# An order of VectorE's work written anew in a four-stage scan, and GpSimd's first operations of a step behind one more wait

## The reference

```python
def _derivative(q, p, drive, coupling, bias):
    i_couple = jnp.tanh(q) @ coupling.T
    dq = q - q ** 3 / 3.0 - p + drive + i_couple + bias
    dp = EPSILON * (q + ALPHA - BETA * p)
    return (dq, dp)
def _rk4_step(q, p, drive, coupling, bias):
    dq1, dp1 = _derivative(q, p, drive, coupling, bias)
    dq2, dp2 = _derivative(q + 0.5 * DT * dq1, p + 0.5 * DT * dp1, drive, coupling, bias)
    dq3, dp3 = _derivative(q + 0.5 * DT * dq2, p + 0.5 * DT * dp2, drive, coupling, bias)
    dq4, dp4 = _derivative(q + DT * dq3, p + DT * dp3, drive, coupling, bias)
    q_next = q + DT / 6.0 * (dq1 + 2 * dq2 + 2 * dq3 + dq4)
    p_next = p + DT / 6.0 * (dp1 + 2 * dp2 + 2 * dp3 + dp4)
    q_next = jnp.clip(q_next, -CLAMP, CLAMP)
    p_next = jnp.clip(p_next, -CLAMP, CLAMP)
    return (q_next, p_next)
```

## Time and profile before

| what | value |
|---|---|
| median of 3 runs | 5511.95 us |
| the profiled execution itself | 5501.18 us |
| its span (first to last instruction) | 5499.4 us |
| TensorE busy | 4413.1 us, 80% |
| VectorE busy | 4183.3 us, 76% |
| ScalarE busy | 2305.9 us, 42% |
| GpSimd busy | 1722.9 us, 31% |

### The profile page before, as it was taken

How to read it: one execution, slowest core, us unless ns; L and a number is a source line. 1 busy time by engine, 2 the same in 40 slices (tenths; PEclk the granted TensorE clock), 3 DMA queues, 4 the chain that set the end, 5 groups by cost and what they waited for, 6 DMA issues and landing times. The chain is left out here.

```text
span 5499.4 us, 212720 instructions
## 1 busy us (share of the span) xinstructions
PE 4413.1 (80%) x78665; PEld 3812.1 (69%) x78665; DVE 4183.3 (76%) x25970; ACT 2305.9 (42%) x10514; POOL 1722.9 (31%) x5965
## 2 busy tenths in 40 slices
PE   6777777777777777777776787699999999969999
PEld 5666666666666666666665566578777787758777
DVE  7999999999999999999995667377777777631123
ACT  3333333333333333333333566255555555432243
POOL 2444444444444444444443221123333323100000
PEclk5555555555555555555557999699999999989999
DMA  2000000000000000000002000322222222131121
GB/s 70 1 1 1 1 1 1 1 1 1 1 1 1 1 1 1 1 1 1 1 1 78 32 21 17 117 73 73 81 76 85 81 74 65 46 137 47 39 100 39
DMA packets 145838, 187.93 MB, mean 34 GB/s; under 512 B 9372, under 2 KB 75492, under 8 KB 145288
## 3 DMA queue, kind: packets, MB, share of 16 engines
q1 hardware_dynamic: 140800, 182.67, 10.0%
q0 software_dynamic: 624, 0.75, 0.1%
q10 hardware_dynamic: 3992, 0.17, 0.0%
HBM read 143.67 MB, written 39.90 MB: 33 GB/s over the span
## 5 line engine op out<-in xcount | busy, mean ns | idle before, releaser
L211 PE MATMUL bank<-tanh_parts,w_lo 128*128 128x4 f16 x32768 | 1208.3, 169 | 756.6 <-ACT tanh_parts L168 755.4
L211 PEld LDWEIGHTS bank<-tanh_parts,w_lo 128*128 128x128 f16 x32768 | 1033.6, 105 | 941.5 <-ACT tanh_parts L168 940.5
L168 ACT ACTIVATE tanh_parts<-ys 128x8 f16<-128x8 f32 x4096 | 857.5, 209 | 1801.2 <-DVE ys L298 1800.2
L219 PE MATMUL bank<-tanh_parts,w_hi 128*128 128x8 f16 x32768 | 1200.7, 173 | 2.9 <-issue 2.9
L219 PEld LDWEIGHTS bank<-tanh_parts,w_hi 128*128 128x128 f16 x32768 | 1059.5, 104 | 3.0 <-issue 3.0
L298 DVE TENSOR_TENSOR_SCAN ys<-mix,bank 128x24 f32<-128x24 f32 x4096 | 805.4, 202 | 125.3 <-PE bank L219 25.3
L169 ACT ACTIVATE tanh_full<-ys 128x8 f32<-128x8 f32 x4096 | 804.0, 196 | 0.0
L290 DVE TENSOR_TENSOR tanh_parts<-tanh_full,tanh_parts 128x8 f16<-128x8 f32 x4096 | 704.0, 172 | 1.3 <-ACT tanh_full L169 0.7
L1256 POOL TENSOR_TENSOR t_w_qk<-t_raw_qk,t_w_qk 128x512 fp32r<-128x512 f32 x128 | 168.1, 1335 | 765.0 <-ACT t_w_qk L1420 765.0
L475 PE MATMUL t_bank<-t_x,t_w_qk 128*128 128x512 f32 x1536 | 361.5, 391 | 12.8 <-DVE t_x L1676 12.8
L475 PEld LDWEIGHTS t_bank<-t_x,t_w_qk 128*128 128x128 f32 x1536 | 290.1, 189 | 73.9 <-DVE t_x L1676 13.5
(11 more groups left out here) (232 smaller groups left out, 9103.6 us busy)
## 6 DMA issues: line engine op xcount, KB each, us to landing
t_raw_qk<-L_cond_qkv_w_dram SPq DMA_DIRECT2D x128, 256.0 KB, 3.3
t_raw_vo<-L_cond_qkv_w_dram SPq DMA_DIRECT2D x16, 1024.0 KB, 5.1
t_raw_vo<-L_cond_out_w_dram SPq DMA_DIRECT2D x16, 1024.0 KB, 5.3
n<-t_parts SPq DMA_DIRECT2D x14, 1024.0 KB, 6.6
g_raw<-L_cond_ffn_w_dram SPq DMA_DIRECT2D x8, 1024.0 KB, 9.9
g_x<-n SPq DMA_DIRECT2D x8, 1024.0 KB, 8.7
ada_w<-L_cond_ada_w_dram SPq DMA_DIRECT2D x4, 1536.0 KB, 10.7
t_x<-n SPq DMA_DIRECT2D x6, 1024.0 KB, 6.9
```

Of the source, the lines that this page charges most:

```text
L168: act.activation(tanh_parts[:, u, at, :, 0], ys[:, s, at, :, 2], ACT.Tanh, scale=1.0 / SCALE).then_inc(s_th, 1)
L211: pe.matmul(sums[:, :, 2], w_lo[:, w_of, k, m * P:(m + 1) * P], tanh_parts[:, u, k, :, 0], start=(m % 2 == 0 and k == 0), stop=False, skip ...
L219: last = pe.matmul(sums[:, :, 1:3], w_hi[:, w_of, k, m * P:(m + 1) * P], tanh_parts[:, u, k], start=False, stop=(m % 2 == 1 and k == C - 1 ...
```

## The change

On VectorE:

- Stage 0: `known` (net times H plus q) is no longer worked out ahead of the base. The gain is folded into `cub` and `slope`, so the base is net times H plus slope. `known_0` is made at the start of stage 1 instead.
- Stage 1: the two parts of `known`, `rate`, `third_1` and `p_2` change places; `rate` now stands behind the base. `twice` goes between the two scans, and the third `known` to the start of stage 2.
- Stage 3: `rate_3` stands ahead of `cub`; the last `thirds` is folded into `slope`, and the base becomes a `tensor_tensor` of slope and known. The clip of p moves from between the two scans to before them.
- `result`: the wait for the base is written behind the wait for `s_mm`, and in stages 0, 1 and 3.
- 45 instructions per step in place of 46.

On GpSimd: the first product `gq` waits for `s_rate` as well (the rate of stage 0), and with it the second product, the trace copy and the sum behind it.

```diff
@@ -98,7 +98,7 @@
         slope = sb("slope", [P, C, B], F32)
         known = sb("known", [P, STAGES, C, B], F32)
         twice = sb("twice", [P, C, B], F32)
-        thirds = sb("thirds", [P, STAGES, C, B], F32)
+        thirds = sb("thirds", [P, STAGES - 1, C, B], F32)

         mix = sb("mix", [P, C, B, 3], F32)
         gq = sb("gq", [P, 2, C, B], F32)
@@ -295,38 +295,38 @@
                 u, to = s % 2, (s + 1) % STAGES
                 for half, at in enumerate(HALVES):
                     v.wait_ge(s_mm, t * 2 * STAGES + (2 * s + half + 1))
+                    if half == 0 and s != 2:
+                        after("base")
                     v.tensor_tensor_scan(ys[:, to, at].rearrange("p c b n -> p (c b n)"), mix[:, at].rearrange("p c b n -> p (c b n)"),
                                          banks[2 * u + half][:, 0:C // 2 * B * 3], 0.0, ALU.mult, ALU.add).then_inc(s_q, 1)
                     if half == 0 and between is not None:
                         between()

-            def cubed(y):
-                own("cub", stt(cub[:, :, :], y, -1.0 / (3.0 * SCALE * SCALE), y, ALU.mult, ALU.mult))
-
-            def sloped(y):
+            def cubed(y, gain=1.0):
+                own("cub", stt(cub[:, :, :], y, -gain / (3.0 * SCALE * SCALE), y, ALU.mult, ALU.mult))
+
+            def sloped(y, first=1.0):
                 after("cub")
-                own("slope", stt(slope[:, :, :], cub[:, :, :], 1.0, y, ALU.add, ALU.mult))
+                own("slope", stt(slope[:, :, :], cub[:, :, :], first, y, ALU.add, ALU.mult))

             def based(s, of):
                 own("base", stt(mix[:, :, :, 1], slope[:, :, :], GAIN[s], of))

             y1, y2, y3 = [ys[:, s, :, :, 2] for s in (1, 2, 3)]
+

             def stage_0(t):
                 v.wait_ge(s_q, t * 2 * STAGES + 2)
                 v.tensor_scalar(q[:, :, :], ys[:, 0, :, :, 2], -CLAMP * SCALE, CLAMP * SCALE, ALU.max, ALU.min).then_inc(s_clip, 1)
                 low_part(t, 0, 0)
                 v.wait_ge(s_clip, t + 1)
-                cubed(q[:, :, :])
+                cubed(q[:, :, :], GAIN[0])
                 low_part(t, 0, 1)
+                sloped(q[:, :, :], 1.0 + GAIN[0])
                 v.wait_ge(s_net, t + 1)
-                own("known", stt(known[:, 0], net[:, :, :], H, q[:, :, :]))
-                sloped(q[:, :, :])
-                v.wait_ge(s_p, t + 1)
                 stt(rate[:, 0], p[:, :, :], -BETA, q[:, :, :]).then_inc(s_rate, 1)
                 after("slope")
-                based(0, known[:, 0])
-                after("base")
+                own("base", stt(mix[:, :, :, 1], net[:, :, :], H, slope[:, :, :]))

                 def between():
                     v.wait_ge(s_rate, t * 3 + 1)
@@ -334,37 +334,35 @@
                 result(t, 0, between)

             def stage_1(t):
-                own("known", stt(known[:, 1], rate[:, 0], -EPSILON * H * H, known[:, 0]))
+                own("known_0", stt(known[:, 0], net[:, :, :], H, q[:, :, :]))
                 v.wait_ge(s_q, t * 2 * STAGES + 4)
                 cubed(y1)
-                after("p_1")
-                stt(rate[:, 1], ps_[:, 1], -BETA, y1).then_inc(s_rate, 1)
+                after("known_0")
+                own("known", stt(known[:, 1], rate[:, 0], -EPSILON * H * H, known[:, 0]))
                 low_part(t, 1, 0)
                 sloped(y1)
                 low_part(t, 1, 1)
                 after("slope")
                 based(1, known[:, 1])
+                stt(rate[:, 1], ps_[:, 1], -BETA, y1).then_inc(s_rate, 1)
+                v.wait_ge(s_third, t + 1)
+                own("third_1", stt(thirds[:, 1], y1, THIRD, thirds[:, 0]))
                 v.wait_ge(s_rate, t * 3 + 2)
                 own("p_2", stt(ps_[:, 2], rate[:, 1], EPSILON * H, p[:, :, :]))
-                v.wait_ge(s_third, t + 1)
-                own("third_1", stt(thirds[:, 1], y1, THIRD, thirds[:, 0]))
-                after("base")
-                own("twice", stt(twice[:, :, :], net[:, :, :], 2 * H, q[:, :, :]))

                 def between():
-                    after("twice")
-                    own("known", stt(known[:, 2], rate[:, 1], -2 * EPSILON * H * H, twice[:, :, :]))
+                    own("twice", stt(twice[:, :, :], net[:, :, :], 2 * H, q[:, :, :]))
                 result(t, 1, between)

             def stage_2(t):
+                after("twice")
+                own("known", stt(known[:, 2], rate[:, 1], -2 * EPSILON * H * H, twice[:, :, :]))
                 v.wait_ge(s_q, t * 2 * STAGES + 6)
                 cubed(y2)
-                after("p_2")
                 stt(rate[:, 2], ps_[:, 2], -BETA, y2).then_inc(s_rate, 1)
                 low_part(t, 2, 0)
                 sloped(y2)
                 low_part(t, 2, 1)
-                after("third_1")
                 own("third_2", stt(thirds[:, 2], y2, 2 * THIRD, thirds[:, 1]))
                 after("slope")
                 based(2, known[:, 2])
@@ -376,24 +374,19 @@

             def stage_3(t):
                 v.wait_ge(s_q, t * 2 * STAGES + 8)
-                cubed(y3)
                 own("rate_3", stt(rate[:, 3], ps_[:, 3], -BETA, y3))
+                cubed(y3, GAIN[3])
                 low_part(t, 3, 0)
-                sloped(y3)
+                sloped(y3, THIRD + GAIN[3])
                 low_part(t, 3, 1)
-                after("late")
-                own("known", stt(thirds[:, 3], y3, THIRD, known[:, 3]))
                 v.wait_ge(s_psum, t + 1)
-                after("rate_3")
                 own("moved", stt(p_new[:, :, :], rate[:, 3], EPSILON * H / 3, p_sum[:, :, :]))
-                after("known")
-                based(3, thirds[:, 3])
-                after("base")
-
-                def between():
-                    v.tensor_scalar(p[:, :, :], p_new[:, :, :], (-CLAMP - SHIFT_P) * SCALE, (CLAMP - SHIFT_P) * SCALE,
-                                    ALU.max, ALU.min).then_inc(s_p, 1)
-                result(t, 3, between)
+                after("slope")
+                own("base", v.tensor_tensor(mix[:, :, :, 1], slope[:, :, :], known[:, 3], ALU.add))
+                after("moved")
+                v.tensor_scalar(p[:, :, :], p_new[:, :, :], (-CLAMP - SHIFT_P) * SCALE, (CLAMP - SHIFT_P) * SCALE,
+                                ALU.max, ALU.min).then_inc(s_p, 1)
+                result(t, 3)

             for t in range(T):
                 stage_0(t)
@@ -435,6 +428,7 @@
                 g.wait_ge(s_p, t + 1)
                 tt(net[:, :, :], drive_now[:, :, :], p[:, :, :], ALU.subtract).then_inc(s_net, 1)
                 g.wait_ge(s_clip, t + 1)
+                g.wait_ge(s_rate, t * 3 + 1)
                 own(tt(gq[:, 0], q[:, :, :], by_rest, ALU.mult))
                 g.wait_ge(s_net, t + 1)
                 of_net = own(tt(gq[:, 1], net[:, :, :], by_third_h, ALU.mult))
```

## The result

The changed kernel takes 5448.72 us (median of 4 runs, 5446.01 to 5453.77) against 5511.47 before (5508.94 to 5513.26): ratio 0.9888, 95% interval 0.987 to 0.9905, 62.8 us less. The forecast was 5439 us in a range of 5419 to 5468.

The account below looks back on a forecast made before the run. The prediction took the scan's ring (scan, tanh, matmuls, scan) at half clock, VectorE 93% busy, as the bound. Terms -69 -13 +12 -3 = -73 us took the profiled 5501.2 to 5428, plus 10.8 gives 5439 us, range 5419 to 5468.

Parts of the forecast that it names:

- The waits: First scans of stages 0 and 3: s_mm rides on the scan, the base wait stands alone at no cost; -69 us.
- The collision in stage 3: With rate_3 first, cub starts level with or ahead of GpSimd's drive_now and escapes its stretch; -13 us.
- The cube at 0.23: Stage 3: cub taking 0.24 us was listed as showing the prediction wrong.
- the first rival: GpSimd strikes more, cub of stage 3 losing to drive_now or cub of stage 1 hit; 5459 to 5475 us, chance 0.2.
- The chain in stage 3: Stage 3: cub 0.09 us later delays slope and low part 1, scan at 1.14 over a floor of 1.12; +12 us.
- Stage 1: A later gp spares low part 1, gain 0.028; hits by GpSimd's moved products cost 0.023 us per step; net -3 us.
- The 46th instruction: VectorE's step: removing one instruction was counted at nothing.
- the slow rivals: Two slower cases: s_mm's wait stands alone, 5543 us, chance 0.04; a full lock, 5531 us, chance 0.03.
- the one by which the lone wait would be that for `s_mm`: First scans of stages 0, 1 and 3: s_mm always gets its own instruction; +31 us, 5543, chance 0.04.
- The full lock: Stage 0: GpSimd's second product holds off p_1 to its end, 0.18 us per step; +92 us, 5531, chance 0.03.
- the ring: The scan phase's repeating chain of each stage: scan, tanh, matmuls, scan.

Follow-up runs that it names:

- e1: The changed kernel with the waits ahead of the first scan of stages 0, 1 and 3 in the old order, base before s_mm: 5555.95 us, ratio 1.0089.
- e4: The kernel before with s_mm written ahead of the base wait in stages 0 and 3, nothing else: 5525.86 us, ratio 1.0031.
- e2: The changed kernel without GpSimd's wait for the rate of stage 0, so VectorE's new order alone: 5477.23 us, ratio 0.995.
- e5: The changed kernel with GpSimd's copy of the next drive waiting until both low parts of stage 3 are written: 5434.40 us, ratio 0.9854.
- e9: The changed kernel with a late drive copy, cub first in stage 3 and the base ahead of moved, 48 entries per step: 5410.09 us, ratio 0.9818.
- e10: The changed kernel with one more wait, for rate_3 ahead of moved, 49 entries per step on VectorE: 5460.81 us, ratio 0.9912.
- e3: The kernel before with GpSimd's wait for the rate of stage 0 and nothing else: 5495.41 us, ratio 0.9968.

## Why the prediction was right, and where it was not

The sum was right to 10 us of 73 by the medians (62.8), to 17 by the stages of the scan (56.3), and its largest term for its reason. The other three terms were wrong and partly made up for each other: two in stage 3 were too good by about 18 and 5 us, the one in stage 1 too bad by 13. That part of the closeness is luck.

- **The waits** (-69). The mechanism is shown by e1. In stage 3 the full 0.07 came (the scan 0.37 behind low part 1, formerly 0.44). Its reason, that the wait written first rides on the instruction, holds in e1, e4 and the changed kernel. In stage 0 the prediction wrote "with the lone wait behind it the scan can go at 2017.17", counting 0.09 from the base to the scan. The four pairs of rows in the changed kernel, e2 and e4 give 0.10 to 0.11. The mean gain of stage 0 is 58 ns instead of 67 and the gain of its median 52, the difference being the vanished stalls. The exchange alone does not bring it: in e4, where the base is as late as before, it costs.
- **The collision in stage 3** (-13). This step failed: "cub starts about 0.01 earlier than rate does now, level with or ahead of the copy, and I expect it to win". I had given the rate a push of 0.09 as in second place; in first place, behind the wait for the state, it pushes the next by 0.10 as cub did (2003.29, 2003.39). cub starts 13 to 14 ns behind the copy, where the rate had started 14 behind it, and was struck in 383 of the 384 steps in which the copy lies there (in every fourth step it comes 0.37 us later). The cube at 0.23 was one of the prediction's own signs of being wrong. That was the first rival's mechanism, given 0.2. Before, the rate was struck in 298 steps, six in ten, so this term was a loss and not a gain: 85 strikes more at the 60 ns by which a struck stage 3 is longer (1447 against 1387) are, by estimate, 5 us. e5 shows what all strikes cost: 46 ns per step.
- **The chain in stage 3** (+12). Right in kind and too small. cub a tenth later makes slope and low part 1 late; in the steps that are not hit stage 3 takes 1387 ns, against 1353 without a lone wait or collision in e9: 34 instead of 23.
- **Stage 1** (-3). It gained 31 ns, 16 us: all that the struck low part 1 had cost and 3 ns more, and the strike on cub or known that I put against it did not come. `thirds` started at 2000.47, 0.10 ahead of cub, which took its usual 0.18.
- **The 46th instruction** "at nothing". Its removal was worth the 6.4 us of the 25 long stages, by the place at which every 128th entry falls (e10). This cost was in the trace of before, in the waits of the scan for TensorE, and I did not ask what they were (the row of `--waits` over the scan):

```profile
DVE ys L298 <- PE bank L219: 22.4, 130, 0.5
```

Of the 130 only 8 belong to long stages, those of 0.4 to 0.5 us; the others are 0.15 to 0.16 us ahead of stage 3's scan in ordinary steps. The other 17 long stages are not in this row.

Of the slow rivals, the one by which the lone wait would be that for `s_mm` is e1: it priced 5543, e1 gave 5556. The full lock did not come. GpSimd's second product started at 2000.16 and takes 0.22; `p_1` started at 2000.26, inside it, took 0.15, and the second scan stood at 2000.34, 0.21 behind the first. By this rule of "SBUF — State Buffer" in the Trainium skill ("SBUF: two separate sides") `p_1` would have waited to 2000.38; the trace does not bear it out at this size. Nor does the one that starts first always keep its time: in e3 `gp` started first, by up to 8 ns, and it was `gp` that was stretched.

The two halves of the change are not additive: GpSimd's wait alone brings 16 us (e3), VectorE's order alone 34 (5511.5 to 5477.2), both 63. Its wait does two different things: in the old order it frees low part 1 of stage 1 (e3), which the new order does by itself (stage 1 is at 1353 in e2); in the new order it keeps GpSimd's operations off the base of stage 0, which has to be written 0.10 before the scan (e2, 45 ns).

## What to carry to other kernels

Where two waits stand ahead of an instruction on the ring, write the one that is met last first, so that it rides on the instruction, and see that the other is met 0.10 us earlier; if it can't be, the exchange costs as much as it brings or more (e4, 66 ns in stage 0). In a ring of 1.4 us, GpSimd's short operations cost by where they fall: move them by a wait away from the two or three instructions that the ring needs, and check the new place in the trace, since ten nanoseconds decide. And when one entry more in a written-out queue costs more than it should, look for late instructions at a fixed distance in the queue (128 entries here): where they fall in a step depends on the number of entries per step, lone waits among them.

## What was not expected of the hardware

- One wait per step more, met long before, cost 12.9 us over 512 steps (e10, 49 entries per step against 48), of which the scan in the trace shows 7.6. The stalls, 44 of 2048 stages and 0.2 us each, all begin at the same one of every 128 entries of VectorE; in the kernel before, all 25 do.
- Of two short instructions of VectorE and GpSimd with SBUF operands that start close together, one keeps its usual time and the other is stretched, VectorE's by 0.03 (the rate in e2, 0.20 for 0.17) to 0.06 us or GpSimd's from 0.20 or 0.22 to 0.25. Beside a `gp`, a low part is spared at up to 11 ns behind it and stretched from 19 ns on; beside `drive_now`, cub and rate went either way at 12 to 15 ns, and in e1 the rate was struck at 1 to 10.
- A wait of VectorE that stands alone puts the next instruction 0.10 to 0.11 us behind the end of the awaited write (base to scan in the changed kernel, e2 and e4), where one that rides on the instruction leaves 0.03 (slope to base of stage 0, in the same kernels).
